# Mixture-of-experts stage: accumulators carried in the gathered rows of two tables, in place of accumulating scatters

## The reference, cut to what matters

```python
h = _layernorm(x) * (1 + cb) + sb
scores = softmax(h @ Wr)                    # 4096 tokens x 8 experts
G, idx = top_k(scores.T, 1024)              # each expert takes 1024 tokens
X_in = h[idx]
hid = gelu(einsum('ekd,edh->ekh', X_in, W1) + b1)
X_e = einsum('ekh,ehd->ekd', hid, W2) + b2
out = zeros(4096, 128).at[idx].add(G * X_e) # a token may be taken by several experts
x = x + gb * out
```

## Time and profile before

| | us |
|---|---|
| median of 3 runs | 1290.49 |
| lowest and highest | 1288.48 and 1291.82 |
| span of the profiled execution, first to last instruction | 1295.1 |
| attention of layer 0 | about 0 to 600 |
| router | about 602 to 692 |
| lists, then experts | about 692 to 712, 712 to 941 |
| attention of layer 1 | about 941 to 1145 |
| feed-forward of layer 1 | to the end |

### The profile page before, as it was taken

One profiled execution on the slowest core, in us unless ns is written; L12 is line 12 of the kernel. 1 busy time (PEld: TensorE's weight loads), 2 busy tenths in 40 slices (PEclk: granted clock), 3 DMA queues, 4 the chain that ended last, 5 costly groups with the idle time before them and its releaser, 6 DMA issues. The chain is left out here.

```text
span 1295.1 us, 25137 instructions
## 1 busy us (share of the span) xinstructions
PE 975.8 (75%) x8604; PEld 662.5 (51%) x8604; DVE 805.3 (62%) x1683; ACT 639.2 (49%) x2132; POOL 430.4 (33%) x332
## 2 busy tenths in 40 slices
PE   6779998989899999985613769747348787867665
PEld 3456565656656565664503556534225454545454
DVE  5777758687777767564657514112136878559995
ACT  3565767767676767671101323112038777643322
POOL 2334333333342423321000857886611312200221
PEclk9789899999999998987555789888759999868967
DMA  6564343434443434431402123445310000000000
GB/s 198 150 182 107 92 123 88 119 96 113 102 113 100 113 83 107 104 91 42 102 0 62 45 59 69 61 73 129 31 66 1 1 2 1 1 1 9 17 17 25
DMA packets 89009, 93.62 MB, mean 72 GB/s; under 512 B 18800, under 2 KB 62304, under 8 KB 88944
## 3 DMA queue, kind: packets, MB, share of 16 engines
q1 hardware_dynamic: 78576, 84.12, 24.7%
q0 software_dynamic: 10368, 8.66, 4.7%
HBM read 24.36 MB, written 10.70 MB: 27 GB/s over the span
## 5 line engine op out<-in xcount | busy, mean ns | idle before, releaser
L835 POOL TENSOR_TENSOR qk_cos<-qk_raw,const 128x512 f32<-128x512 f32 x128 | 183.2, 1432 | 313.0 <-ACT qk_raw L589 313.0
L575 ACT ACTIVATE prob<-psS,neg_max 128x96 f32<-128x96 f32 x512 | 167.9, 342 | 86.5 <-DVE neg_max L670 85.7
L442 PE MATMUL psQ<-a_xnT,weights 128*128 128x512 f32 x250 | 146.0, 668 | 2.1 <-ACT a_xnT L621 1.4
L550 PEld LDWEIGHTS psO<-probT,v_windows 96*64 96x64 f32 x2048 | 73.7, 143 | 142.6 <-ACT probT L649 121.1
L550 PE MATMUL psO<-probT,v_windows 96*64 96x64 f32 x2048 | 91.8, 235 | 43.9 <-ACT probT L649 43.9
L685 DVE TENSOR_TENSOR qk_roped<-qk_cos,qk_swapped 128x512 f32<-128x512 f32 x128 | 119.0, 929 | 5.9 <-DVE qk_swapped L676 5.5
L1508 POOL DMA_INDIRECT sums<-ex_y,ex_index x64 | 97.6, 1525 | 39.5 <-issue 23.5
L1497 POOL DMA_INDIRECT ex_rows<-rows,ex_index x64 | 67.1, 1048 | 121.8 <-DMA ex_index<-lists 102.6
L575 ACT ACTIVATION_READ_ACCUMULATOR prob<-psS,neg_max 128x1 f32 x512 | 105.4, 206 | 0.0
L1442 ACT ACTIVATE ex_hidden<-ex_psH,ex_b 128x512 f32<-128x512 f32 x64 | 43.7, 687 | 114.4 <-PE ex_psH L1401 59.7
L649 ACT COPY probT<-psT 96x512 f32<-96x512 f32 x128 | 76.8, 600 | 46.5 <-PE psT L530 46.5
(11 more groups left out here) (317 smaller groups left out, 1936.2 us busy)
## 6 DMA issues: line engine op xcount, KB each, us to landing
qk_swapped<-qk_raw SPq DMA_DIRECT2D x512, 64.0 KB, 2.0
v_windows<-v_tok SPq DMA_DIRECT2D x32, 384.0 KB, 4.4
v_windows<-v_tok SPq DMA_DIRECT2D x32, 256.0 KB, 3.6
mod<-mod_rows SPq DMA_DIRECT2D x12, 512.0 KB, 6.0
ex_w<-in_L_ffn_W SPq DMA_DIRECT2D x16, 256.0 KB
v_windows<-v_tok SPq DMA_DIRECT2D x32, 96.0 KB, 2.1
rows<-rt_h SPq DMA_DIRECT2D x8, 256.0 KB, 2.4
sums<-rt_zeros SPq DMA_DIRECT2D x8, 256.0 KB, 2.7
```

Of the source, the lines that this page charges most:

```text
L442: last = nc.tensor.matmul(bank, k.wqkvT[:, col:col + P], xnT[:, :], start=True, stop=True)
L550: ins = nc.tensor.matmul(psO[D * j:D * j + D, i * P + a * HALF:i * P + (a + 1) * HALF], vw[:, par, a, t, hd], probT[:, 2 * j + i, a * HALF ...
L575: last = nc.scalar.activation(prob[:, s, 2 * j + i, :], psS[:, s, j, i * KW:(i + 1) * KW], ACT.Exp, bias=nmax[:, s, 2 * j + i:2 * j + i + ...
L835: nc.gpsimd.tensor_tensor(rcos[:, half, :], raw[:, half, :], k.const[:, K_COS:K_COS + T], ALU.mult).then_inc(cos_done, 1)
```

## The change

A table row becomes 264 values (1056 bytes): the token's 128 values, its 8 scores, and 128 values of an accumulator. There are two such tables in DRAM, one for the even and one for the odd experts. Both get the tokens and the scores; their accumulator columns are filled with zeros by two DMAs of 2 MB each, which SP starts in units 9 and 11 of the first sequence of layer 0's attention, from a tile of zeros that DVE sets at its start. A gather brings the accumulators along, DVE adds the expert's weighted output to them on chip, and the scatter writes the whole row back without adding. So the gather of expert e+2 has to wait until the scatter of e has landed (both use the same table), and it now stands behind that scatter in POOL's order; scatters of neighbouring experts no longer wait for each other. The copies of `keep` are gone, all lists are loaded before the loop, all eight experts are written out, and PE's `turn_x` stands at the start of each expert in place of between up and down. Layer 1 loads both accumulator planes and adds them: for the first two sequences on DVE, for the others on POOL.

```diff
-ROW = C + E0
+ROW = C + E0 + C
+PLANES = 2
 # phase_attention0
+        blank = k.mod1[:, 0, 0, :]
+            nc.vector.memset(blank, 0.0).then_inc(blanked, 1)
+                        if u in (9, 11):
+                            sp.wait_ge(blanked, 1)
+                            plane = k.rows[(u - 9) // 2].rearrange("(n p) c -> p n c", p=P)[:, :, C + E0:ROW]
+                            sp.dma_start(plane, blank.unsqueeze(1).to_broadcast([P, NT, C])).then_inc(ld_late, 16)
 # phase_router
-            nc.gpsimd.memset(zeros[:, :, :], 0.0).then_inc(zeroed, 1)
-                sp.dma_start(rows[b][:, :, 0:C], h[:, s2, :, :]).then_inc(h_stored[s2], 16)
-                sp.wait_ge(zeroed, 1)
-                sp.dma_start(sums[b], zeros[:, :, :]).then_inc(cleared, 16)
+                for r in rows:
+                    sp.dma_start(r[b][:, :, 0:C], h[:, s2, :, :]).then_inc(h_stored[s2], 16)
-            sp.dma_start(k.rows.rearrange("(n p) c -> p n c", p=P)[:, :, C:ROW], s[:, :, :]).then_inc(scores_stored, 16)
+            for r in k.rows:
+                sp.dma_start(r.rearrange("(n p) c -> p n c", p=P)[:, :, C:C + E0], s[:, :, :]).then_inc(scores_stored, 16)
-                wait(dve, h_stored[s2], turn * 16)
+                wait(dve, h_stored[s2], turn * 16 * PLANES)
 # phase_experts, PE
+            for e in range(E0):
+                turn_x(e)
+                if e == E0 - 2:
+                    mod.turn(pe)
+                    mod.multiply(pe)
+                up(e)
+                down(e)
 # ACT: the wait for kept is gone, the bias is read from k.b1T
 # SP
             for g in range(GROUPS):
+                pair = slice(g * GROUP, (g + 1) * GROUP)
                 sp.wait_ge(ids_ready, g + 1)
+                sp.dma_start(k.lists[pair].rearrange("e (a l) -> (e a) l", l=SPLIT), ids[:, g, :]).then_inc(list_stored, 16)
+                sp.wait_ge(list_stored, 16 * (g + 1))
+                sp.dma_start(index[:, pair, :], k.lists[pair].rearrange("e (p s) -> p e s", s=SLOTS)).then_inc(index_ld, 16)
+                sp.wait_ge(index_ld, 16 * (g + 1))
+            for e in range(2, E0):
+                weights(e)
 # POOL
+            def gather(e):
+                pool.wait_ge(index_ld, 16 * (e // GROUP + 1))
                 wait(pool, x_turned, e - 1)
-                wait(pool, kept, e - 1)
+                wait(pool, scattered[e % 2], 16 * SLOTS * (e // 2))
...
+            def scatter(e):
-                wait(pool, scattered[1 - par], 16 * SLOTS * (turn + par))
                 for n in range(SLOTS):
                     if n % 4 == 0:
                         pool.wait_ge(y_ready, 2 * e + 1 + n // 4)
                         pool.nop(nofuse=True)
+                    nc.gpsimd.indirect_dma_start(k.rows[e % 2], bass.IndirectOffsetOnAxis(ap=index[:, e, n:n + 1], axis=0),
+                                                 rows[:, e % 2, n, :], None, compute_op=ALU.bypass).then_inc(scattered[e % 2], 16)
+            gather(0)
+            gather(1)
+            for e in range(E0):
+                scatter(e)
+                if e + 2 < E0:
+                    gather(e + 2)
 # DVE
-            def keep(e, par, turn):
...
+            for e in range(E0):
+                take_x(e)
...
                 for i in range(2):
...
+                    nc.vector.tensor_tensor(y[:, slots, :], y[:, slots, :],
+                                            rows[:, e % 2, slots, C + e:C + e + 1].to_broadcast([P, 4, C]), ALU.mult).then_inc(weighted, 1)
+                    dve.wait_ge(weighted, 2 * e + 1 + i)
+                    acc = rows[:, e % 2, slots, C + E0:ROW]
+                    nc.vector.tensor_tensor(acc, acc, y[:, slots, :], ALU.add).then_inc(y_ready, 1)
+                if e == 1:
                     mod.silu(dve)
                     weights1.quantise(dve)
 # phase_attention1
+                for r, to in zip(k.rows, (k.total, plane)):
+                    sp.dma_start(to[:, lo:hi, :, :].rearrange("p b t c -> p (b t) c"),
+                                 r[lo * T:hi * T, C + E0:ROW].rearrange("(t p) c -> p t c", p=P)).then_inc(sums_ld[i], 16)
+            def add_planes(b):
+                nc.gpsimd.tensor_tensor(k.total[:, b, :, :], k.total[:, b, :, :], plane[:, b, :, :], ALU.add).then_inc(planes_added, 1)
             norm.root_bias(pool, 1)
+            pool.wait_ge(sums_ld[1], 16 * PLANES)
+            add_planes(2)
             def body(b, par, first, next1, next2):
                 if next2:
                     norm.root_bias(pool, b + 2)
+                if b + 3 < B:
+                    add_planes(b + 3)
 # DVE, add_experts
+                if b < 2:
+                    dve.wait_ge(own.sem, own.mark(nc.vector.tensor_tensor(k.total[:, b, :, :], k.total[:, b, :, :],
+                                                                          plane[:, b, :, :], ALU.add)))
+                else:
+                    dve.wait_ge(planes_added, b - 1)
```

More of the change, by code:

```diff
@@ L1339, in phase_experts @@
             sem(n) for n in ("ranked", "highs", "lows", "weighed", "listed", "ids", "list_stored"))
[L1340 to L1342 removed]
+        w_ld, gathered, scattered = ([sem(f"{n}{i}") for i in range(2)] for n in ("w_ld", "gathered", "scattered"))
+        index_ld = sem("index_ld")
+        x_turned, hT_act, hT_dve, up_done, gelu_done, down_done, psY_read, weighted, y_ready = (
+            sem(n) for n in ("x_turned", "hT_act", "hT_dve", "up", "gelu", "down", "psY_read", "weighted", "y"))
         spare = lambda buf, pattern: buf.rearrange(pattern).bitcast(F32)
@@ L1351, in phase_experts @@
         block = ctx.enter_context(nc.Block())
[L1353 to L1361, removed]
         @block.tensor
@@ L1400, in body, with down @@
                         wait(pe, gelu_done, e * 2 * KD + n - 1)
-                        nc.tensor.matmul(psH[n % 2][:, :], w1[:, par, d * P:(d + 1) * P], hT[:, par, i, :],
+                        nc.tensor.matmul(psH[n % 2][:, :], w1[:, e % 2, d * P:(d + 1) * P], hT[:, e % 2, i, :],
                                          start=True, stop=True).then_inc(up_done, 1)
-                if not (last_pair and e == E0 - 1):
-                    turn_x(e + 1, 1 - par, turn + par)
-                wait(pe, psY_read, 2 * e)
+            def down(e):
                 for n in range(SLOTS):
@@ L1507, in scatter @@
                         pool.nop(nofuse=True)
-                    nc.gpsimd.indirect_dma_start(k.sums, bass.IndirectOffsetOnAxis(ap=index2[:, par, n:n + 1], axis=0),
-                                                 y[:, par, n, :], None, compute_op=ALU.bypass if written else ALU.add).then_inc(scattered[par], 16)
-            gather(0, 0, 0)
-            gather(1, 1, 0)
-            def body(e, par, turn, first, last_pair):
-                if not last_pair:
-                    gather(e + 2, par, turn + 1)
-                scatter(e, par, turn)
-            turns(pool, body)
+                    nc.gpsimd.indirect_dma_start(k.rows[e % 2], bass.IndirectOffsetOnAxis(ap=index[:, e, n:n + 1], axis=0),
[6 more added lines that the diff above has]
+                    gather(e + 2)
             for par in range(2):
@@ L1572, in _, with take_x @@
             take_list(GROUPS - 1)
-            def keep(e, par, turn):
-                dve.wait_ge(gathered[par], 16 * SLOTS * (turn + 1))
-                wait(dve, scattered[par], 16 * SLOTS * turn)
-                nc.vector.tensor_copy(b1[:, par, :], k.b1T[:, bass.ds(e * KD, KD)])
-                nc.vector.tensor_copy(gate[:, par, :], rows[:, par, :, bass.ds(C + e, 1)].rearrange("p s o -> p (s o)"))
-                nc.vector.tensor_copy(index2[:, par, :], index[:, par, :]).then_inc(kept, 1)
+            def take_x(e):
                 dve.wait_ge(x_turned, e + 1)
-                nc.vector.tensor_copy(hT[:, par, 1, :], psX[:, 1, :]).then_inc(hT_dve, 1)
-            def body(e, par, turn, first, last_pair):
-                if last_pair and e == E0 - 2:
+                nc.vector.tensor_copy(hT[:, e % 2, 1, :], psX[:, 1, :]).then_inc(hT_dve, 1)
+            for e in range(E0):
+                take_x(e)
+                if e == E0 - 2:
                     mod.finish(dve)
-                if not (last_pair and e == E0 - 1):
-                    keep(e + 1, 1 - par, turn + par)
                 for i in range(2):
@@ L1618, in phase_attention1 @@
         mul = sb("a1_mul", [P, TILES, C])
-        sums_ld = [sem(f"sums_ld{i}") for i in range(2)]
+        sums_ld, planes_added = [sem(f"sums_ld{i}") for i in range(2)], sem("planes_added")
+        plane = sb("a1_plane", [P, B, TILES, C])
         h, hT = sb("a1_h", [P, TILES, C]), sb("a1_hT", [C, T])
@@ L2192, in build @@
         k.mod, k.mod1 = sb("mod", [P, MODS, B, C]), sb("mod1", [P, MODS, B, C])
+        k.rows = [nc.dram_tensor(f"rows{i}", (B * T, ROW), F32, kind="Internal").ap() for i in range(PLANES)]
         phase_attention0(nc, k)
```

123 lines of the change are left out of this document (38 added, 85 removed).

## The result

The kernel after takes 1292.6 us (median of 20 runs, 1287.2 to 1300.0), the kernel before 1287.6 (20 runs, 1282.3 to 1292.5): ratio 1.0041, 95% interval 1.0024 to 1.0058. It is slower by 0.4%, 5 us, where 10 us of gain were forecast. The time lies in the range given, the direction is wrong.

A forecast was written before the change was run, and what follows sets the result against it. POOL's issuing of indirect DMAs was taken to bound the experts. -23.3 + 3.3 + 1 + 6.6 + 0.5 = -11.9 us, rounded to a gain of 10.5 and carried to the median: 1280 us, range 1269 to 1303.

The forecast's parts named there:

- the -23.3 of the experts: Expert stage: last scatter issued at 912.2 in place of 935.5 us, a gain of 23.3 us.
- Experts: the start: Expert 0: its down runs unbroken, so scatter 0 starts at 748.1 in place of 753.3 us.
- the end of expert 7: Last expert: nothing covers its chain, so scatter 7 follows the end of its gather by 18.3 us.
- the fills: Layer 0's first sequence: swaps queue behind two 2 MB DMAs, losing 2.9 and 3.7 us, together +6.6 (0 to 11).
- the router: Router: waiting for two stores in place of one holds `rt_h` a little, +0.5 us.
- start and cycle: Experts: scatter 0 at 748.1 us, then 22.3 us per expert: scatters 10.3, landing wait 1.9, gathers 10.1.
- layer 1: Layer 1: loading and adding two planes costs +3.3 us at its start, POOL's additions +1 (0 to 4).
- broken down phases: Rival, experts: gathers break PE's down, about 24 us lost, giving 1304 us, or 1292 if half heal; chance 0.27.
- fresh code: Rival, experts: written-out experts cause the breaks, so all eight show one, about 1305 us; chance 0.05.
- fills cost twice: Rival, layer 0: SP stays blocked while a fill flows, 2 x 8 in place of 6.6 us, 1289; chance 0.13.
- the forecast's own range: Whole kernel: 1271 to 1287 us, from the ends for fills, landing and layer 1's start.

The follow-up runs named there:

- e1: The kernel before, unchanged, run again for a second profile: 1286.0 us, ratio 0.9983.
- e2: The kernel after, unchanged, run again for a second profile: 1291.8 us, ratio 1.0035 to the kernel before.
- e11: The kernel after with fills moved to the router's search and layer 1's modulation-row spread held until expert 7's rows are turned: 1275.3 us, ratio 0.9925.
- e3: The kernel after with its two fills moved from layer 0 to the router's search: 1283.9 us, ratio 0.9967 to the kernel before.
- e4: The kernel before with only the two fills added, into two tables that nobody reads: 1297.3 us, ratio 1.0073.
- e9: The kernel before with layer 1's modulation-row spread held until expert 7's rows are turned: 1288.0 us, ratio 1.0015.

## Why the prediction was wrong, step by step

**The base of the sum: the step that failed.** The term that failed is the -23.3 of the experts, taken against 935.5, the end of one execution, and carried over to the median. That execution had two breaks of PE, worth 9.4 us of its stretch (223.4 against e1's 214.0). The first was booked as a gain of the change in "Experts: the start" (4.0 of the 5.2 there: e1's scatter 0 comes 37.2 us after gather 0, 41.2 in that execution); the second went in through the end, 935.5. Neither is in any of the three other profiles with before's expert stage. The sum did note a distance of 4.6 us, but between a span and a time; time against time it is 1296.9 less 1287.6, 9.3 us, the size of the breaks. With 935.5 replaced by 926.1 the sum is -2.5 in place of -11.9: that alone would have made the forecast "the same". The other 7 us, from -2.5 to the +4.5 added up below, are the end of expert 7 (+5.7), the fills (+1.9), the router (+1.5) and the start and cycle (+1.2), less 3.3 that layer 1 did not cost. The text even built two rivals on the breaks, *broken down phases* (0.27) and *fresh code* (0.05), and did not ask whether they recur. Both fell: e1, e2 and after run unbroken, after with a gather beside down and all eight experts written out.

**Experts: the start and the cycle.** Right. Scatter 0 comes 35.7 us after gather 0, 36.0 were forecast; issues 1.29 and 1.25 as forecast for wide rows; the landing wait 2.4 lay inside its ends (1.4, 2.5), at the upper one, where the Trainium skill's "DMA: Bandwidth & Descriptors", the section on the anatomy of one DMA, had put its estimate of 2.3: here page and trace agree. Gather 7, of as many bytes an issue, lands 1.8 to 1.9 us after its last issue where no spread flows beside it, below the estimate. Scatter 0 to scatter 6 takes 137.3 us, 135.8 forecast.

**The end of expert 7.** Sized 18.3, measured 24.0: +5.7. The forecast's pieces were right (e11: 17.9), but the sum put a landing of 1.6 and an up of 7.8 into them without asking what else SP sends at that time: with the spread beside it the landing takes 5.3 and up 9.5. It followed the index loads and the fills; the spread, not touched by the diff, met gather 7 only because the new order issues that gather later. The second half is PE: in the kernel before, the turn lay between up and down, PE waited 2.6 us for gathered rows in all, and its idle time was inside up, 25.3 us behind ACT's Gelu; after, it waits before each expert from the third on, and what follows, turn and up, runs at the lower clock in part. The grouped rows, before (e1), then after (busy us and mean ns of one, then idle us before them and what ended it):

```profile
L1401 PE MATMUL ex_psH<-ex_hT,ex_w 128*128 128x512 f32 x128 | 69.5, 683 | 26.1 <-ACT ex_hidden L1442 25.3 <-ACT ex_hT L1432 0.8
L1388 PE MATMUL ex_psX<-const,ex_rows 128*128 128x128 f32 x64 | 9.4, 295 | 2.6 <-DMA ex_rows<-rows,ex_index 2.6
```

```profile
L1392 PE MATMUL ex_psH<-ex_hT,ex_w 128*128 128x512 f32 x128 | 71.4, 705 | 5.1 <-issue 4.3 <-ACT ex_hT L1429 0.8
L1381 PE MATMUL ex_psX<-const,ex_rows 128*128 128x128 f32 x64 | 13.1, 371 | 28.8 <-DMA ex_rows<-rows,ex_index 28.7
```

The prediction took `turn_x` as moved within the cover. So it is for the middle experts, where up takes 8.3 to 10.3 us in after and no scatter is later for it; for the last there is no cover.

**The fills.** Sized 6.6, measured 8 (e2 less e3) and 9 (e4 less before). The mechanism was right and the first wait was hit (2.9, measured 2.94); the second was 5.93 where 3.7 were forecast, on the idea that the first delay gives some back. It does not. The text gave SP one issue per fill and nothing more; the trace shows the next issue held for 4.75 and 5.62 us. So the rival *fills cost twice* was farther off in size than the forecast (16 us, against 8 to 9 measured and 6.6 forecast) but partly right in its picture: SP is held behind a fill, for less than the fill's 7 us, and with the next issue only; those after it take 1.3 us and less.

**The router.** Sized 0.5. From POOL's first root of the router to gather 0 the kernel before takes 108.8, 107.3 and 107.5 us (its profile, e1, e9), after and its variants with two tables 109.9 to 111.7, three tables 113.0: about +2 to 3 per table. Two stores must now land before `rt_h` is free: DVE waits 2.7 us for them in after and in e2, 5.6 with three tables and nothing before; about the size of the difference. **Layer 1.** Sized +3.3 and +1: its first normalisation starts 13.3 us after the last scatter in e1 and 14.1 in after, and from the last scatter to the end of the span it is 358.4 and 358.7 (359.6 in e2). +1 in all; the additions on POOL cost nothing that shows.

Together: fills +8.5, router +2, experts -7, layer 1 +1, that is +4.5, against 4.9 and 3.7 measured. **The range** held by luck: it reached to 1303 for broken downs that no run after the change shows, and the forecast's own range ended at 1287.

## What to carry to other kernels

Check the profiled execution against the timed runs before summing on it, and look for stalls in it that repeat in no other expert, sequence or tile: until such a stall is seen again it is no gain that a change can take, and no rule to build a rival on. When a change delays a transfer, list what every queue sends in the new place, the queues that the diff leaves alone too, and look at the one instance that has no cover, the last. A large transfer whose place is free goes where nobody waits, or is cut into pieces between the small ones.

## What the runs showed of the hardware

- A wide plain scatter (1056 bytes a row) issues in 0.98 us, a wide gather in 0.95, as those of 512 and 544 bytes did; an adding scatter takes 1.56. Adding costs, width does not.
- Gather 7's rows land 1.8 to 1.9 us after its last issue with nothing beside them and 5.2 to 5.4 when 3 MB of plain DMAs flow beside them (four and six profiles); gather 6's land after 2.9 to 3.7 us when 512 KB of weights are issued 1.2 us before its end (three profiles).
- 4 MB of fills cost 8 us as two transfers and 2.3 as sixteen, in the same stretch of work.
- The first DMA that SP issues behind a 2 MB fill takes 4.4 to 6.3 us to issue in place of 0.6 (six such issues in after, e2 and e4).
- After 6.5 us of waiting PE was granted 0.50 of its clock, after 0.5 us still 1.00. The same eight transposes take 1.97 and 1.1 us. After waits of about 4 us both lengths occur (1.09 and 1.97 in after), with an up of 9.1 to 9.5 us behind either.
- Of three profiles with the same expert stage as before's first one, none repeats its two breaks of PE; an execution can hold 9.4 us of stall that is not in the usual run.
